# A graph layer on one core: node scales, last row tiles and their reload as 112 and 13 rows, second adjacency block asked for last

## What is computed

```python
norm = edge_weight * rsqrt(deg_out[src] * deg_in[dst] + EPS)
def _gcn_layer(x, W, b, src, dst, norm, n_nodes):
    xt = x @ W
    msg = xt[src] * norm[:, None]
    agg = segment_sum(msg, dst, num_segments=n_nodes)
    return relu(agg + b)
h6 = _gcn_layer(xn, W6, b6, ...)
h7 = _gcn_layer(h6, W7, b7, ...)
x = x + h7 @ Wp + bp + mix(xn)
x = x + ffn(layernorm(x))
```

## Time and profile before

| | |
|---|---|
| median of 3 runs | 3709.88 us |
| profiled execution, own time | 3675.28 us |
| its span | 3673.5 us |
| PE busy | 3014.1 us (82%) |
| POOL busy | 2169.9 us (59%) |
| DVE busy | 1801.7 us (49%) |
| ACT busy | 1146.4 us (31%) |
| mean DMA rate | 140 GB/s |
| mean granted TensorE clock | 0.908 |
| PE idle before its first product of layer two | 24.32 us |
| POOL idle before its first gather of layer two | 36.23 us |
| POOL idle before its first gather of layer one | 26.50 us |

### The profile page before, as it was taken

One profiled execution on the slowest core, in us unless ns is written; L12 is line 12 of the kernel. 1 busy time (PEld: TensorE's weight loads), 2 busy tenths in 40 slices (PEclk: granted clock), 3 DMA queues, 4 the chain that ended last, 5 costly groups with the idle time before them and its releaser, 6 DMA issues.

```text
span 3673.5 us, 51374 instructions
## 1 busy us (share of the span) xinstructions
PE 3014.1 (82%) x16152; PEld 1995.3 (54%) x16152; DVE 1801.7 (49%) x4528; ACT 1146.4 (31%) x4063; POOL 2169.9 (59%) x2090
## 2 busy tenths in 40 slices
PE   4778836888888888888875888888888878888998
PEld 3445524555555555555553555556555546555666
DVE  9989835666666666666541332223212324232334
ACT  5788734444444444344320110002000101012211
POOL 4766656766767677676764666666666666630000
PEclk8899968999999999999987989889888989889999
DMA  4331134454545545445465534654554554533221
GB/s 119 99 102 59 52 78 135 152 164 137 179 141 165 153 140 178 136 152 163 129 208 176 150 105 156 202 187 149 193 191 153 187 159 152 189 112 101 81 77 48
DMA packets 219168, 515.12 MB, mean 140 GB/s; under 512 B 62470, under 2 KB 129461, under 8 KB 207799
## 3 DMA queue, kind: packets, MB, share of 16 engines
q0 software_dynamic: 88704, 243.35, 23.2%
q1 hardware_dynamic: 123683, 261.95, 20.9%
q10 hardware_dynamic: 6500, 6.40, 0.6%
HBM read 384.49 MB, written 127.07 MB: 139 GB/s over the span
## 4 chain that ended last, share of the span: by engine, by line
PE 39%; another core or an unknown queue 5%; issue 5%; DVE 2%; DMA 2%; SPq 1%; ACT 1%; DVEq 0%; ACTq 0%; POOL 0%; POOLq 0%
PE ps L709 17%; PE ps L883 5%; PE ps L670 5%; PE ps L896 5%; PE ps L683 3%; PE ps L816 1%; PE ps L828 1%; PE ps L831 1%; DMA xb<-t 1%; SPq L2054 0%; DMA x2d<-accb 0%; PE ps L648 0%; PE ps L719 0%; PE ps L840 0%
## 5 line engine op out<-in xcount | busy, mean ns | idle before, releaser
L1975 POOL DMA_INDIRECT ringb<-t,src x1848 | 1860.5, 1007 | 939.2 <-issue 499.7
L709 PE MATMUL ps<-xb,ab 125*128 125x256 f32 (+1 forms) x4700 | 1251.2, 405 | 101.1 <-issue 97.7
L709 PEld LDWEIGHTS ps<-xb,ab 125*128 125x128 f32 x4700 | 924.4, 201 | 384.6 <-issue 228.1
L683 PE MATMUL ps<-mlb 128*125 128x300 f32 x1260 | 474.4, 468 | 158.7 <-issue 93.8
L1752 ACT ACTIVATE ab<-ps 125x250 f32 x724 | 294.5, 407 | 753.0 <-PE ps L683 350.4
L670 PE MATMUL ps<-ringb,Sb 128*32 128x257 f32 (+1 forms) x3696 | 374.6, 415 | 89.1 <-issue 60.1
L683 PEld LDWEIGHTS ps<-mlb 128*125 128x125 f32 x1260 | 224.2, 201 | 320.3 <-issue 261.1
L1948 POOL TENSOR_TENSOR ab<-ab,wn 128x100 f32<-128x100 f32 x201 | 274.1, 1369 | 167.6 <-DVE ab L1096 167.6
L610 PE MATMUL ps<-ab 128*50 128x125 f32 x3228 | 222.2, 285 | 132.8 <-ACT ab L1672 47.0
L1282 DVE TENSOR_TENSOR mlb<-iof,rel 128x900 f32<-128x900 f32 (+1 forms) x231 | 232.3, 1005 | 170.2 <-remote 95.0
L1672 ACT ACTIVATE ab<-ab,wn 128x50 f32<-128x50 f32 x1212 | 286.7, 327 | 20.8 <-DVE ab L1096 20.7
(11 more groups left out here) (246 smaller groups left out, 2697.6 us busy)
## 6 DMA issues: line engine op xcount, KB each, us to landing
ad<-ab SPq DMA_DIRECT2D x42, 1600.0 KB
ab<-ad SPq DMA_DIRECT2D x42, 1600.0 KB
ringb<-t,src POOLq DMA_INDIRECT x1848
kvd<-mlb SPq DMA_DIRECT2D x50, 256.0 KB, 2.1
kvb<-kvd SPq DMA_DIRECT2D x50, 256.0 KB
x2t<-mlb SPq DMA_DIRECT2D x13, 500.0 KB
xb<-x2t SPq DMA_DIRECT2D x13, 500.0 KB, 8.2
xb<-in_x SPq DMA_DIRECT2D x10, 625.0 KB
```

The lines of the kernel that those rows point to most:

```text
L683: e.matmul(PS[bank_of(t)][0:R, 0:HR], low[:, slot_of(t), :], high[:, slot_of(t), :], start=True, stop=True).then_inc(s_bld, 1)
L709: ins = e.matmul(PS[dense_bank(L, d)][:, 0:wd], lhs, X[0:R, k, 0:wd], start=k == 0, stop=k == NT - 1)
L1975: e.indirect_dma_start(msg[:, slot * QT + k, 0:width], None, table, bass.IndirectOffsetOnAxis(src[:, t:t + 1], 0)).then_inc(s_g[slot], 16)
```

## The change

Three kinds of DMA on SP and ACT are cut into two along the partitions, rows 0 to 111 and rows 112 to 124 (WHOLE = 125 - 125 % 16 = 112): the store of the scales, the stores of row tiles 47 to 49, and all six reload pieces. The semaphore counts that others wait for are raised to match (stores_of counts two DMAs for each tile from KEPT on). Row tiles 0 to 46 and the reciprocal roots are stored as before. load_A(1) moves from a step inside the loop, where it stood ahead of the reload of tiles 40-46, to behind the reload of tiles 20-24.

```diff
+WHOLE = R - R % 16
...
+        def stores_of(n, parity):
+
+            return loads_of(n, parity) + sum(1 for i in range(KEPT, n) if i % 2 == parity)
...
-                        e.wait_ge(l_xr, 16 * len(X_PIECES))
+                        e.wait_ge(l_xr, 32 * len(X_PIECES))
...
-                    e.wait_ge(l_xl, 16)
+                    e.wait_ge(l_xl, 32)
...
-                e.dma_start(tile_rows(t2, i), row).then_inc(l_t2[i % 2], 16)
+                if i < KEPT:
+                    e.dma_start(tile_rows(t2, i), row).then_inc(l_t2[i % 2], 16)
+                else:
+                    e.dma_start(tile_rows(t2, i)[0:WHOLE], row[0:WHOLE]).then_inc(l_t2[i % 2], 16)
+                    e.dma_start(tile_rows(t2, i)[WHOLE:R], row[WHOLE:R]).then_inc(l_t2[i % 2], 16)
...
-            e.wait_ge(l_dego, 16)
+            e.wait_ge(l_dego, 32)
...
-                        e.wait_ge(l_t2[k], 16 * loads_of(NT, k))
+                        e.wait_ge(l_t2[k], 16 * stores_of(NT, k))
...
-            e.dma_start(t1[:, D:TW].rearrange("(t p) c -> p t c", p=R), scl[0:R, :, :],
-                        allow_slow_non_contiguous=True).then_inc(l_dego, 16)
+            roots = t1[:, D:TW].rearrange("(t p) c -> p t c", p=R)
+            for a_, b_ in ((0, WHOLE), (WHOLE, R)):
+                e.dma_start(roots[a_:b_], scl[a_:b_, :, :], allow_slow_non_contiguous=True).then_inc(l_dego, 16)
...
-                    e.wait_ge(l_t2[k], 16 * loads_of(stored, k))
-                e.dma_start(X[0:R, i0:i1, 0:D], t2[R * i0:R * i1, :].rearrange("(t p) d -> p t d", p=R)).then_inc(done, 16)
+                    e.wait_ge(l_t2[k], 16 * stores_of(stored, k))
+                rows = t2[R * i0:R * i1, :].rearrange("(t p) d -> p t d", p=R)
+                for a_, b_ in ((0, WHOLE), (WHOLE, R)):
+                    e.dma_start(X[a_:b_, i0:i1, 0:D], rows[a_:b_]).then_inc(done, 16)
...
-                for c in range(2):
-                    if s == max(at for at, m in MULT_AT[0].items() if (ND - 2 + c, NT - 1) in m) + 1:
-                        load_A(c)
+                if s == max(at for at, m in MULT_AT[0].items() if (ND - 2, NT - 1) in m) + 1:
+                    load_A(0)
...
             reload_X(20, 25, NT, l_xl)
+            load_A(1)
             e.dma_start(rsd_in.rearrange("(t p) -> p t", p=R), rdi[0:R, :], allow_slow_non_contiguous=True).then_inc(l_dego, 16)
-            e.wait_ge(l_dego, 32)
+            e.wait_ge(l_dego, 48)
```

## The result

The changed kernel takes 3692.08 us (median of 6 runs, 3683.78 to 3697.48) against 3709.95 us for the kernel before (6 runs beside it, 3706.78 to 3718.16). The ratio is 0.9946, interval 0.993 to 0.9962: 20 us less, between 14 and 26 (the two medians lie 17.9 us apart). The forecast was a sum of 23.2 us and 3687 us.

The account below looks back on a forecast made before the run. PE was taken to wait for data at the starts of both layers, behind slow 125-row transfers. 18.8 + 5.0 - 0.6 = 23.2 us takes the median 3709.88 to 3687 us (sum's bounds 3676 to 3695); range 3674 to 3702.

Parts of the forecast that it names:

- 112 rows spread over all 16 engines: Reload pieces as 112 + 13 rows: ten tiles take 3.1 us instead of 11.5 us on five engines.
- Rival B: The split brings nothing, only the order: PE starts layer two near 2003, scales gain 0, time 3701 us; chance 10%.
- The rate taken for the pieces, 407 GB/s: Rate of 128-row blocks and weights in 1915 to 1920, assumed for the cut reload pieces instead of 111 GB/s.
- PE's start, 18.8 us: First product of layer two at 1993.3 instead of 2012.06: ACT's copy ends 1988.4, plus 4.92 us between piece's landing and product.
- Piece five ahead of the block: Reload before layer two: piece five lands at the latest at 1977, before 1988.4, so five pieces leave PE's path.
- Gathers, "11.3 us earlier": Start of layer two: POOL starts gathers at 1984 instead of 1995.3, with enough lead that PE never waits.
- Second block last, 0 us: Layer two: adjacency block issued at about 1984 lands by 2014, before PE's first column of it at 2027.7; costs 0 us.
- Scales, 5.0 us: Start of layer one: POOL starts 9.9 us earlier, but DVE's mask limits the first step's gain to 5.0 us.
- 14.9 x 5/16 = 4.7: Scales' store: 14.9 us of moving (17.0 less 2.1 landing) becomes 4.7 on 16 engines, 7.1 us with the second issue.
- ACT's extra issues, -0.6 us: Last row tile stores: three splits cost ACT 0.27 us each, at most two between tiles, so 0.6 us lost.
- C: Gathers pace layer two, so only POOL's 11.3 us count, and 5.0 or less in front: 3694 to 3698 us; chance 15%.
- E: PE catches up with another wait in layer two, or layer one's start does not carry: 3705 us; chance 7%.

## Why the prediction was right, point by point

*The mechanism, "112 rows spread over all 16 engines".* Right as far as the shares tell: they rose from 0.34 to about 1, and the cuts at 124 and 120 rows show that the row count decides it. Rival B (only the order brings something) is refuted by the pieces alone, which bring 11.8 us without the order. The warning of the Trainium skill ("DMA: Bandwidth & Descriptors", "Rules for kernel authors", that transfers to disjoint partition halves serialize) gives as its reason that both halves run over all 16 engines anyway. With 125 rows the uncut transfer did not, by its share of 0.34, and the cut paid.

*The rate taken for the pieces, 407 GB/s.* Too high: 206 to 223 GB/s in the two stretches of the change shown, 194 to 253 in the five from 1950 to 1975, with gathers and stores beside them. At such rates a piece of ten tiles (1.28 MB) takes 5 to 6.6 us, not 3.1. The stretch from which 407 was read moved gathers too, 0.58 of its 2.03 MB. It cost nothing, since the pieces are over by 1990, 17 us before PE is ready.

*PE's start, 18.8 us (bounds 15.4 and 23.7).* Measured 16.5 us in the pair of profiles, 18.7 against the second profile of the kernel before. The term that was off is the one taken from the row of 4.92 us: from the end of ACT's copy it is 6.77 us here, and 4.3 us in the kernel with the pieces alone (1995.81 less the copy's end at 1991.53), where no block moves at that time. So in the order of before 4.92 would have been about right. Two things were missed: that the order was not free, and that the gap to be removed itself varies by 9 us between executions.

*Piece five ahead of the block.* Counted in with the first term, rightly; but it does nothing once the pieces are cut. The change with and without it gives 0.9949 and 0.9947, on two chips of the same kind.

*Gathers, "11.3 us earlier".* POOL's first gather comes 2.3 us after the last store's issue instead of 15.1, so 12.8 us earlier. The reason given for the 15.1, the block's packets in front, is only part of it: with the order alone 8.0 us are left, and with the pieces alone and the store whole 3.3. The slow pieces held the store up. What the cut of the last three row stores adds was never run by itself; by these numbers it is about 1 us. POOL had enough lead: in the change its first stop comes at 2035.14, well after PE's first step of gathers at 2026.85.

*Second block last, 0 us.* No wait for it showed up at its first product, as forecast. Its 2 us came at another place, above.

*Scales, 5.0 us (bounds 0 and 9.9).* 3.7 us in the profile after, but that is the upper end. From the scales' store to PE's first product it is 24.3 to 25.4 us in the four profiles with the old store and 20.6 to 23.1 in the nine cut at 112 or 120 rows: 2.5 us on average. The cut alone brought 0.7 us, which can't be told from none. "14.9 x 5/16 = 4.7" was not the error. In 475 to 480 the share is now 1.23 at 10 GB/s, where the earlier trace rows has 0.53 at 4:

```profile
475.00:480.00 5.00, 0.00 (x0) 0.00 (x0) 4.19 (x5) 0.00 (x0) 0.00 (x0) 0.84 1.23 10
```

The DMA queues in the same stretch (packets, MB, share), before and then after:

```profile
q1 hardware_dynamic: 2651, 0.02, 53.0%
```

```profile
q1 hardware_dynamic: 6006, 0.05, 123.1%
```

The store has 6250 pairs. Before, their packets ran until some 14 us after the issue; now all but a few have moved after 6.6. But POOL does not start then. Its first gather comes about when the next two transfers on SP's queue end (kvb<-kvd, 256 KB each): their packets end at 11.0 us and POOL starts at 11.4, before at 17.1 and 17.0, and within 1 us of each other in every other profile. So the term that was off is the 2.1 us for landing, which was 2.7 before and is 4.8 here; why POOL starts with the end of those loads stays open.

The second error is that DVE's wait of 4.98 us would go away whole. In eight of the nine cut profiles 2.0 to 2.1 us of it stay, and PE's first product follows DVE's first instruction by 7.0 to 7.1 us in each of them (7.06 here), whenever POOL began: the gather that runs while DVE starts takes 2.3 to 3.3 us instead of 0.95 (2.56 in the row above), and the next one starts 3.46 us after DVE's first instruction. DVE itself starts 14.3 to 14.7 us after the store with the old store and 13.6 to 16.0 with the cut one. So POOL's earlier start is mostly lost beside DVE; why that gather is longer no run tests.

*ACT's extra issues, -0.6 us.* They cost nothing: the last two tiles are stored 1998.65 - 1994.91 = 3.74 us apart, as before (1980.20 - 1976.46 in the timeline of ACT). ACT waits for PE and DVE between them (2.12 and 0.85 us).

*The sum, 23.2 us.* With the measured terms it is 16.5 + 3.7 = 20.2 us in the pair of profiles, the timed difference is 20 us (14 to 26). On the other chips the change gave 13.3 us (8.5 to 18.1) and 17.2 us (11.8 to 22.3), so 23.2 was on the high side everywhere, and outside the interval on both of these chips. That 20.2 and 20 agree so well is partly luck: against the three gaps of the old reload the first term is 16.5, 18.7 or 25.3 us, and the scales' cut alone brought 0.7. The mechanism is shown, the sum is good to some 10 us.

*Rivals C and E.* C, that POOL becomes the bound, describes the faster chips, where it was the bound already; 3694 to 3698 was its price, and the result of 3692 does not tell it apart from the forecast. Of E, a gain given back, there may be a trace: in both profiles of the change on slower chips, and in the one with the pieces alone, PE stands still some 2.7 to 7.1 us in all between single products shortly after its start, for no reason that the profile shows; in the four with a late start it is under 1.5 us, and on faster chips none. Timeline of PE in the change:

```profile
2030.39 0.38 PE L714 MATMUL ps<-xb,ab 125*128 125x256 f32 x1 [0.94 <-issue]
2032.50 0.58 PE L714 MATMUL ps<-xb,ab 125*128 125x256 f32 x1 [1.74 <-issue]
2033.91 4.94 PE L714 MATMUL ps<-xb,ab 125*128 125x256 f32 x11 [0.83 <-issue]
```

It could explain a part of why the pieces alone close the gap by 19 us or more and win 11.8. But such stops are not special to this place. Over all of layer two PE's stops of this kind before L709 and L670 (or the same lines of the other kernels), less the one at the start, add up to 106 and 116 us in the two profiles before, 117 with the order alone, 130 with the scales alone, 112 with the pieces alone and 125 and 123 in the change. So the traces don't show that a shorter rest before the start causes them, and where the gain went stays open. So does the order alone: it wins 8.1 us (3.7 to 12.5) with a gap of 25.3 + 1.4 us, which is 1 to 10 us less than the three gaps of the old reload.

## What to carry to other kernels

Look at the share of the DMA engines in a stretch where one transfer moves alone: 0.34 at 111 GB/s was enough to suspect that a 125-row transfer used a third of them. Cut such a transfer where its first part has a large divisor up to 16 (112 or 120, not 124), and only where somebody waits for it: of four edits, the reload pieces carried nearly all (11.8 of 13.3 us on one chip), the order added nothing that can be told from none once they were cut, the scales alone brought nothing clear, and the last row stores were never tried alone. Before counting on an earlier start, look at which engine's first instruction the next step really follows: at the start of layer one it was DVE's. When a wait for data goes, price what stands behind it on the same engine (here 5 to 7.5 us after a jump) by a place where it is seen, and ask which transfers now run beside it.

## What the hardware showed that was not expected

- Transfers whose share of the 16 DMA engines is about 1 moved 206 to 223 GB/s for the pieces of 112 + 13 rows (1 KB runs), while the stretches with blocks of 128 rows (12.8 KB runs), gathers beside them, moved 404 to 407. The share says that engines are occupied, not that the rate is at its top. Packets of 1 KB took 50 ns each on average in the stretch at 0.34 and 112 GB/s, and 72 and 89 ns in the two of the change at 223 and 206. That is why a share three times as high brought only twice the rate. What makes them longer was not tested.
- PE's standstill after the jump into layer two is 5.0 to 5.4 us without and 7.0 to 7.7 us with a 3.3 MB load beside it, in nine profiles without exception.
- A gather that runs while DVE starts at layer one takes 2.3 to 3.3 us instead of 0.95, in all nine profiles with the scales cut at 112 or 120 rows.
- The same program takes 3684 us on some chips and 3373 on others. TensorE's mean granted clock is 0.90 to 0.91 on the first and 0.93 on the second, and the engine that paces layer two is another by its waits: PE on the first, POOL on the second. On the first, PE also stops between products for nothing that the profile shows, 106 to 130 us in layer two in seven profiles; on the second there are no such stops after its start, in seven profiles. What sets the chips apart no run shows.
